# W2 and the second batch's x loaded by ScalarE, W2 turned in beats 2 to 5, two buffers filled behind the first norm

## The reference, cut to what matters

```python
x = x + attention(layernorm(x))        # x: 8 x 512 x 128 f32, 16 heads of 8
    # Q, K, V = xn @ W.T + b ; softmax(Q K^T / sqrt(8)) V ; then @ Wo.T + bo
x = x + ffn(layernorm(x))
    # logits = xn2 @ Wr.T + br ; top 2 of 8 experts, softmax over the two
    # expert e: relu(xn2 @ W1[e].T + b1[e]) @ W2[e].T + b2[e]   (128 -> 512 -> 128)
    # layernorm(xn2 + weighted sum of the two) * gamma + beta
```

## Time and profile before

| | us |
|---|---|
| median of 3 runs | 658.61 (655.89 to 659.9) |
| the profiled execution | 660.18 |
| its span, first to last instruction | 658.4 |
| PE, DVE, ACT, POOL busy | 594.1, 486.0, 436.7, 232.7 |

### The profile page before, as it was taken

One profiled execution on the slowest core, in us unless ns is written; L12 is line 12 of the kernel. 1 busy time (PEld: TensorE's weight loads), 2 busy tenths in 40 slices (PEclk: granted clock), 3 DMA queues, 4 the chain that ended last, 5 costly groups with the idle time before them and its releaser, 6 DMA issues.

```text
span 658.4 us, 12760 instructions
## 1 busy us (share of the span) xinstructions
PE 594.1 (90%) x3656; PEld 323.1 (49%) x3656; DVE 486.0 (74%) x1287; ACT 436.7 (66%) x886; POOL 232.7 (35%) x397
## 2 busy tenths in 40 slices
PE   2889999999999999999999999999889699998872
PEld 1634333343344333443343333433689599988730
DVE  3576998998999899999899898992354254444358
ACT  2724788888788788788888887788554244434323
POOL 7110010023322331422422510520777545454545
PEclk9965999999999999999999999999999799999986
DMA  7751802212312303302312311130223222222172
GB/s 202 246 165 35 195 29 76 83 39 82 99 45 81 105 28 97 107 26 79 117 35 75 101 56 27 51 108 1 70 75 110 70 64 67 67 68 65 32 267 116
DMA packets 46622, 56.98 MB, mean 87 GB/s; under 512 B 8366, under 2 KB 25818, under 8 KB 46564
## 3 DMA queue, kind: packets, MB, share of 16 engines
q1 hardware_dynamic: 40580, 45.06, 23.4%
q0 software_dynamic: 4544, 8.53, 3.8%
q10 hardware_dynamic: 1440, 2.69, 1.1%
HBM read 29.28 MB, written 27.16 MB: 86 GB/s over the span
## 4 chain that ended last, share of the span: by engine, by line
PE 60%; DVE 20%; ACT 8%; issue 4%; POOL 3%; DMA 2%; SPq 2%; DVEq 0%; ACTq 0%; POOLq 0%
PE pv_psum L1051 11%; DVE mneg L763 10%; PE st_psum L981 9%; PE s_psum L965 9%; PE y_psum L1526 7%; ACT pt L645 4%; PE side_psum L1013 2%; PE h_psum L1517 2%; PE side_psum L987 2%; PE y_psum L1196 2%; PE h_psum L1518 2%; PE h_psum L1519 2%; PE side_psum L1007 2%; ACT xn L663 2%; DVE split L770 2%
## 5 line engine op out<-in xcount | busy, mean ns | idle before, releaser
L763 DVE TENSOR_REDUCE mneg<-s_psum 128x1 f32<-128x512 f32 x512 | 322.8, 683 | 31.8 <-PE s_psum L965 30.3
L645 ACT ACTIVATE pt<-st_psum 128x512 f32<-128x512 f32 x512 | 279.1, 598 | 68.6 <-PE st_psum L981 63.9
L965 PE MATMUL s_psum<-ks,qs 64*128 64x512 f32 x512 | 204.0, 472 | 3.0 <-DVE mneg L763 1.9
L981 PE MATMUL st_psum<-qs,ks 64*128 64x512 f32 x512 | 194.3, 458 | 8.3 <-ACT pt L645 7.6
L965 PEld LDWEIGHTS s_psum<-ks,qs 64*128 64x128 f32 x512 | 83.2, 190 | 108.7 <-DVE mneg L763 87.0
L1051 PE MATMUL pv_psum<-pt,vst 128*16 128x512 f32 x1024 | 134.4, 598 | 0.0
L981 PEld LDWEIGHTS st_psum<-qs,ks 64*128 64x128 f32 x512 | 79.9, 187 | 52.5 <-ACT pt L645 41.3
L1388 ACT ACTIVATE hid<-h_psum,b1c 128x384 f32<-128x384 f32 x68 | 37.0, 581 | 53.3 <-PE h_psum L1519 53.3
L1353 POOL DMA_INDIRECT results<-res,goal_now x51 | 49.9, 979 | 52.3 <-DVE res L1439 38.2
L505 POOL DMA_INDIRECT sent<-xrow,placeu x56 | 54.5, 973 | 16.3 <-issue 16.3
L1526 PE MATMUL y_psum<-w2t,hid 128*128 128x128 f32 x408 | 48.8, 276 | 0.0
(11 more groups left out here) (214 smaller groups left out, 805.0 us busy)
## 6 DMA issues: line engine op xcount, KB each, us to landing
parts<-split SPq DMA_DIRECT2D x48, 256.0 KB, 3.0
ks<-parts SPq DMA_DIRECT2D x128, 48.0 KB
qs<-parts SPq DMA_DIRECT2D x128, 48.0 KB
lot<-sent SPq DMA_DIRECT2D x18, 198.0 KB, 2.6
sent<-tail SPq DMA_DIRECT2D x16, 198.0 KB, 4.6
xres<-in_L_attn_x_dram SPq DMA_DIRECT2D x8, 256.0 KB, 3.2
pt<-in_L_ffn_W_dram SPq DMA_DIRECT2D x1, 2048.0 KB, 14.1
got<-results SPq DMA_DIRECT2D x8, 256.0 KB, 6.4
```

What stands on the lines that cost most here:

```text
L645: nc.scalar.activation(pt[:, n % PT_SLOTS, (g + 2) % 4, :], st_psum[:, k % ST_BANKS, :], ACT.Exp, scale=SCALE).then_inc(exp_done, 1)
L763: nc.vector.tensor_reduce(mneg[:, (n // 4) % 2, at:at + 1], s_psum[:, k % S_BANKS, :], AX_X, ALU.max, negate=True).then_inc(max_done, 1)
L965: mm(s_psum[:, k % S_BANKS, :], qs[rows, c, P * (n % 4):P * (n % 4) + P], ks[rows, c, g, :], start=True, stop=True).then_inc(s_made, 1)
L981: mm(st_psum[:, k % ST_BANKS, :], ks[rows, c, g, P * (n % 4):P * (n % 4) + P], qs[rows, c, :], start=True, stop=True).then_inc(st_made, 1)
```

## The change

The load of x of batch 1 and that of W2 leave SP's list and are issued by ACT, on ACT's own hardware queue, behind beat -9. W2's transposes and copies move from beats -4 to -1 into beats 2 to 5, two experts a beat, at the end of the beat. DVE waits for `shift_done` of batch 0 before it zeroes `qs` and fills `ks`. ACT's two fills move from beat -10 to the end of beat -5. `load_parts` of the first two quads waits only for DVE's fills, that of the others for ACT's too. (The new loop over `load_parts` issues in the same order as the old one.)

```diff
+W2_LOAD_BEAT = -9
...
 def expert_weights(T):
-    return range(2 * (T + 8), 2 * (T + 8) + 2) if -8 <= T < 0 else ()
+    if -8 <= T < -4:
+        return range(2 * (T + 8), 2 * (T + 8) + 2)
+    if 2 <= T < 6:
+        return range(E + 2 * (T - 2), E + 2 * (T - 2) + 2)
+    return ()
...
@@ sync
-        sp.dma_start(xres[:, TILES:2 * TILES, :], x_tiles[:, 1]).then_inc(x1_loaded, 16)
...
-        sp.dma_start(w2raw, W2.rearrange("e p f -> p e f")).then_inc(w2_loaded, 16)
...
@@ load_parts
-                sp.wait_ge(rows_blank, 4)
+                if c < 2:
+                    sp.wait_ge(first_blank, c + 1)
+                else:
+                    sp.wait_ge(first_blank, 2)
+                    sp.wait_ge(later_blank, c - 1)
...
@@ scalar
-            if T == -10:
+            if T == W2_LOAD_BEAT:
+                act.dma_start(xres[:, TILES:2 * TILES, :], x_tiles[:, 1]).then_inc(x1_loaded, 16)
+                act.dma_start(w2raw, W2.rearrange("e p f -> p e f")).then_inc(w2_loaded, 16)
+            if T == -5:
                 for c in range(2, QUADS):
                     nc.scalar.copy(ks[:, c], ident[:, SHIFT_ROW:P:32].unsqueeze(2).to_broadcast([P, 4, S]))\
-                        .then_inc(rows_blank, 1)
+                        .then_inc(later_blank, 1)
...
@@ vector
         nc.vector.memset(pv_psum[:], 0.0).then_inc(pv_blank, 1)
+        dve.wait_ge(shift_done, 1)
         nc.vector.memset(qs[:].bitcast(U32), 0)
         dve.wait_ge(ident_ready, 1)
         for c in range(2):
             nc.vector.tensor_copy(ks[:, c], ident[:, SHIFT_ROW:P:32].unsqueeze(2).to_broadcast([P, 4, S]))\
-                .then_inc(rows_blank, 1)
+                .then_inc(first_blank, 1)
```

More of the change, by code:

```diff
@@ L327, in attention @@
         sem(n) for n in ("w_turned", "w_ready", "bvb_ready", "cols_made", "cols_ready"))
-    rows_blank, pv_blank = sem("rows_blank"), sem("pv_blank")
+    first_blank, later_blank, pv_blank = sem("first_blank"), sem("later_blank"), sem("pv_blank")
     stats_done, moments_done, vareps_done, rstd_done, xn_done = (
@@ L426, in beat @@
                 load_parts(0, 0)
-                for q in range(QUADS):
+                load_parts(0, 1)
+                for q in range(1, QUADS):
+                    load_parts(q, 0)
                     load_parts(q, 1)
-                    if q + 1 < QUADS:
-                        load_parts(q + 1, 0)
                 sp.dma_start(b1raw, b1.rearrange("e (c p) -> (e c) p", p=P)).then_inc(b1_loaded, 16)
```

## The result

The changed kernel takes **666.14 us** (median of 10, 661.81 to 669.01) against 659.12 for the kernel before, timed beside it (10 runs): ratio 1.0113, interval [1.0083, 1.0142]. It is slower by just over 1%. The forecast was 653.2 us, the range ended at 658.3.

A forecast was written before the change was run, and what follows sets the result against it. Bound: the chain of waits over the first 52 us. At beat 9, -5.5 + 3.0 + 0.4 - 3.3 = -5.4: 654.8 from the profiled 660.18, which lies 1.6 above the median, so 653.2 us; range 649.0 to 658.3.

The forecast's parts named there:

- The wait on DVE: Run-up: POOL's power falls from 4.51 to 1.01 us, ACT normalises at 7.1 us, -3.1 us.
- ACT's list: Run-up: ACT's fills go out, two DMA issues come in; first W1 copy at 20.1 us, -3.6 (-1.1 at an issue of 5.02).
- W2 out of the run-up: Run-up: with no W2 between first W1 copy and batch 1's aggregation, DVE is ready at 28.0 us.
- Is Q back by then: Ahead of beat 0: Q's stores land at 24.1 us, first maximum at 28.5 instead of 33.98, -5.5 us.
- An even split: Q's stores against W2 and x: both queues share 391 GB/s, so Q's stores get 195 GB/s and take 4.0 us.
- W2 in beats 2 and 3: W2's transposes at 1.2 GHz make beats 2 and 3 take 11.2 us instead of 8.2, +3.0 us.
- W2 in beats 4 to 8: PE at 2.4 GHz from beat 4: +0.4 us in beats 4 and 5, -3.3 in beats 6 to 8.
- The gain is what beat 9 moves by: After the run-up: engines run their lists in order, so the whole gain equals beat 9's shift, -5.4 us.
- the clock stays at 1.2 GHz: Rival: clock low to beat 9, beats 2 to 5 take 19.8 us against 13.2; +7.6 against -5.5, 660.7 us; chance 0.12.
- the collision: Rival: W2's load holds ACT or goes ahead of Q's stores; beat 0 only 2 us earlier, 656.6 us; chance 0.15.
- SHIFT of beat 6 is covered: Beat 6: SP's list ends some 3 us earlier, which beats 4 and 5 cover, so the SHIFT DMA costs nothing.

The follow-up runs named there:

- the first experiment: The changed kernel with ACT issuing W2's load behind the last W1 copy (beat -5): 663.79 us, ratio 1.0046.
- the ninth experiment: The changed kernel with SP's eight prefill stores in beat 12 instead of beat 8: 665.05 us, ratio 1.0085.
- the sixth experiment: The changed kernel with x and W2 loaded by SP, plus eight repeated W1 transposes a beat in beats -4, -3, -2, 0 and 1: 661.32 us.
- the sixth to eighth experiments: The sixth; changed kernel with loads on SP, W2 turned as before, ACT's fills last (659.39 us); that with repeated transposes in beats 0 to 5 (659.99 us).
- the fourth experiment: The changed kernel with W2's load behind the last W1 copy and eight repeated W1 transposes a beat in beats -4 to 1: 662.25 us, ratio 0.9985.

## Why the prediction was wrong

Taken by its own steps, at beat 9, from -5.4 to +4.8, and on to the end:

- **The wait on DVE: right.** The power took 1.01 us, ACT normalised at 6.74 (7.1 forecast), K's stores went out at 13.99 ("near 14"). The cover just sufficed: DVE's fills of K took 4.15 us, not 2.29, and with a copy behind them ended at 13.94 with K's low half.
- **ACT's list: right.** Issues of 0.39 and 0.52 us; the feared 5.02 did not come. First W1 copy 19.84 (20.1), ACT's later fills hidden.
- **W2 out of the run-up: right.** DVE ready at 27.74 (28.0), and the first experiment starts beat 0 there.
- **Is Q back by then: the step that failed first.** "An even split" put Q's stores at 24.1; they landed at 29.0, later even than the bound of 27.6 with W2 whole ahead. The split was read from two queues that already both moved. Here one queue had just been given 2 MB, and the other's stores moved 0.02 MB in 4 us. The first maximum came at 32.82 instead of 28.5: **+4.3**. The Trainium skill, "DMA: Bandwidth & Descriptors", Queues, rings and completion order, says that each DMA engine takes turns between the queues that have work for it, by packets. The stretch from 22 us on (0.95 against 1.56 MB) comes nearer to that; the one before does not.
- **W2 in beats 2 and 3: right** (11.4 us against 11.2 at 1.2 GHz).
- **W2 in beats 4 to 8: the second step that failed.** I wrote "PE is then busy nearly throughout, as in the stretch before the clock rose, so I take 2.4 GHz from beat 4". PE was busy 19.74 of 20.10 us, and the clock stayed at 0.50 until 67.2. Beats 4 and 5 took 8.7 us instead of 5.35 (**+3.3**), beats 6 to 8 12.6 instead of 10.2 (**+2.4**). Likeness to one earlier stretch was the whole ground. With PE kept busy ahead of beat 0 and in beats 0 and 1 the clock did not fall before 47.9, and the same work took 12.0 us. The lull at 25 to 32 us was foreseen, but its price was ended at beat 4 on that likeness alone. What brings the clock up again once it is low isn't settled by these runs.
- **"The gain is what beat 9 moves by": failed by 1.9**, in beats 14 and 15. The later beats move with beat 9 only as long as SP's list keeps up; the prefill in beat 8 stands ahead of SHIFT, and the ninth experiment takes the stall away.

The sum is -5.4 + 4.3 + 0.2 + 3.3 + 2.4 + 1.9 = +6.7 against 6.9 measured. Of the rivals, "the clock stays at 1.2 GHz" had beats 2 to 5 right to 0.3 us (19.8 against 20.1), and the collision had its mechanism and its sign: a first maximum after 31, with PE waiting 6.8 us for loads into `qs`. They were given as cases that exclude each other; both came. The low-clock rival's 660.7, plus 4.3 for Q's stores and 1.9 for beats 14 and 15, is 666.9, and that it lies so near the measured 666.14 is in part luck: the rival had 14.5 us for beats 6 to 8, which took 12.6. I gave it 0.12 and left it out of the range. The Trainium skill, "TensorE: Matmul & The Clock Gate", Part 4: PE-mode transpose, spoke for it: transposes, it says, do not count as work toward the full clock. The rival's outcome held, but the rule is not what these runs show: in the sixth experiment repeated transposes alone filled the gap ahead of beat 0, and the granted clock stayed at 1.00; before, W1's and W2's transposes, alone on PE, went from 0.24 us each to 0.13. The trace lists them as plain matrix products, so whether they run in the mode that the Trainium skill means is not shown.

"SHIFT of beat 6 is covered" did no harm in the slow kernel, where PE came there at 57.65. It was wrong all the same: in the sixth to eighth experiments, where PE came there by 49.0, PE waited 2.1 to 2.5 us for SHIFT and beat 6 took 7.9 to 8.1 us, with the clock down; the same beat a batch later takes 3.6 (110.9 to 114.5 in the changed kernel). SP's list is one part of that lateness and the DMA's landing the other: with the list thinned, beat 6 still took 6.7 and 8.0 us. (Two small sums of the forecast are off and change nothing: four transposes at 2.82 for 12 take 0.94 us, not 1.1, and 0.18 and 0.14 make 0.32.)

## What to carry to other kernels

A load moved to another queue still shares the engines with what it was meant to let pass: count the bytes in flight when the store is issued, not the queues. Work taken out of a run-up can leave TensorE idle there and then be paid at half clock elsewhere; price it at both levels, and add the rivals that can come together. Before a gain in front is carried to the end, follow the in-order list of each issuing queue past it, and the landing of what it issues: here the gain was taken back twice on SP's list. A store group moved behind SHIFT cured the second place; at the first, with loads moved to ACT's queue, SHIFT went out earlier and landed more slowly.

## What was not expected of the hardware

- A 2 MB DMA behind another 2 MB on one queue held its issuer 5.02 us; on ACT's queue, behind x's 256 KB, 0.52 us. In eight pieces it held ACT 6.22 us.
- The two fills of K took 4.15 us beside POOL's constants against 2.29 beside its power. Before, the power paid (4.51 us); now DVE does, and POOL's small fill of `vst` beside it took 1.28 us against 0.31. Either way the two slow each other, as I read it; no run took this apart.
- One kernel's times differ with its mean granted clock: the fourth experiment gave 652.1 us at 0.982 and 664.4 at 0.956. When the clock comes back differs as well: at 61.3 us in the ninth experiment, at 67.2 in the changed kernel, with the same program up to there.
- A SHIFT DMA of 8 KB landed 3.50 and 3.56 us after issue with x loaded from SP's list ahead of it, and 4.70 and 4.92 us with x loaded by ACT at the same time.
